# Weighted values of four steps in one block, six probability buffers, low queries in three buffers, maxima planned one step earlier

## The chip, the cores and the metric

The kernel runs on one core of one Trainium2 chip. The metric is the device time of one execution in microseconds (us), the median of several runs.

## The reference

A transformer block on x of 4 x 2048 x 512 in float32: layer norm with modulation, attention with 16 heads of 32 columns and 32 rotary columns shared by all heads, and a feed-forward part. What matters here is the attention:

```python
c_kv = x @ W_kv_down
k_rope = _rotary_apply(c_kv @ W_k_rope, cos, sin)
k = (c_kv @ W_k_up).reshape(Bb, Tt, NH, HD)
v = (c_kv @ W_v_up).reshape(Bb, Tt, NH, HD)
q = (x @ W_q).reshape(Bb, Tt, NH, HD)
q_rope = _rotary_apply(x @ W_q_rope, cos, sin)
scores = jnp.einsum('bqhd,bkhd->bhqk', q, k)
scores = scores + jnp.einsum('bqr,bkr->bqk', q_rope, k_rope)[:, None]
scores = scores / scale
causal = jnp.triu(jnp.ones((Tt, Tt), dtype=bool), k=1)
scores = jnp.where(causal[None, None], -jnp.inf, scores)
w = jax.nn.softmax(scores, axis=-1)
attn = jnp.einsum('bhqk,bkhd->bqhd', w, v).reshape(Bb, Tt, D_MODEL)
```

## The kernel before

The program has three stages one after the other: projection (modulation, layer norm, queries, keys and values, written to DRAM as high and low parts), attention, and feed-forward. The change touches attention alone.

Attention works on 16 units (`NU`), a unit being four heads of one batch. A unit has four chunks of 512 queries (`TCH`), j = 0 to 3, and chunk j has 4(j+1) steps of 128 keys each, so that a unit has 40 steps (`NSTEP`) and the kernel 640. They begin at `FIRST` = 0, 4, 12 and 24. The last four steps of each chunk lie on the diagonal and are 512, 384, 256 and 128 queries wide.

What one step t does:

- **PE, scores** (`scores`, L1194 and L1195). For each of the four heads two matmuls, of the high queries with high and low keys and of the low queries with the high keys. The low queries' buffer `q_b` has one row more, which holds minus the maximum of each query, so that the maximum is subtracted on the way. Three PSUM banks (`SBANKS`) take the scores.
- **ACT** (`exponentials`, L1035) writes the exponentials into one of five probability buffers (`RING`). It waits until PE's values and POOL's sum have read the step that had the buffer.
- **POOL** (`clear_future`, `add`) clears what lies behind the diagonal (L1115) and sums the probabilities of the steps that `SHARE_OF` marks with G into `sum_g` (L1130, L1131, L1134). The steps marked T are summed on PE instead.
- **PE, weighted values** (`weighted_values`, L1201). Each head's values fill 32 columns of the array, so four heads run side by side into `ps_o`; the steps marked T are run again with ones in place of the values, into `ps_d`. This work comes in blocks, `over_two_steps`: at each odd t a block for the steps t-3 and t-2 (`LAG` = 2).
- **The closing** (`close_denominators`), in the block two steps behind a chunk's last one: PE multiplies `sum_g` by ones into `ps_d`. At chunks 0, 2 and 3 it stands first in its block, at chunk 1 last. It needs POOL's last sum of the chunk, and POOL's first sum of the next chunk needs the closing (`closed`).
- **DVE behind the closing**: four reciprocals of `ps_d` (`invert`, L1084) and one scaling (`normalise`, L1088). They are entered in `extras` at fixed steps, two reciprocals at the first step behind the closing, two and the scaling at the second.

The maxima are found ahead of their use, by full-precision scores that are thrown away. PE makes a piece (`maximum`, L1178) of 128 queries by up to 512 keys into one of three banks (`MBANKS`), and DVE reduces it, a plain one at L1071, one on the diagonal at L1074. A piece's matmul waits until DVE has taken the piece three places before. A unit has 160 pieces; the last of a chunk is followed by a turn (L1166, L1065) and by a small DMA that places the maxima in `q_b` (`place_max`).

Where the pieces go is decided at build time. `maximum_plan` deals the pieces of unit u over pairs of steps from step 24 of the unit before to step 21 of its own. `deal` gives a pair a number of pieces that grows with `streams(m)`, PE's work in the pair in matmuls of 512 columns, less `CLOSING` in the pair that begins two steps behind a chunk's first one, where DVE has reciprocals to do:

```python
closes = lambda m: CLOSING * any(FIRST[j] + 2 == 2 * m for j in range(TCH))
share = lambda rho, m: max(0.0, (rho * streams(m) - closes(m)) / (PIECE - rho))
```

Within a step PE spreads the pieces behind its parts (four heads, and the block where there is one), and DVE spreads them between its extras, both in the same order. PE, DVE, ACT and POOL each run their list in order.

SP issues the loads in order, each behind a wait: a chunk's queries for the next unit when its scores are done. Each chunk j has its own `q_a[j]` and `q_b[j]`.

Of the kernel before, what the change touches and what calls it, by code (L numbers as in the profile page):

```python
# [22 lines left out]
P = 128  # L23
# [632 lines left out]
RING = 5  # L656
# [13 lines left out]
ENDS_ON_PE = [owners[-1] == "T" for owners in SHARE_OF]  # L670
OPENED_BY_SUM = ["T" not in owners.rstrip("T") for owners in SHARE_OF]
# [71 lines left out]
def maximum_plan():  # L743
# [3 lines left out]
    for u in range(NU):  # L747
# [14 lines left out]
    return plan  # L762

# [33 lines left out]
def operand_loads(sp, scratch, ops, k_b=None, kb_in=None):  # L797
# [34 lines left out]
def attention(nc, keep, scratch, ops, dram):  # L832


    with ExitStack() as ctx:
# [7 lines left out]
        ops["q_b"] += [sb(f"q_b{j}", [2 * HD + 1, GH, CH], F32R) for j in range(1, TCH)]  # L843
# [40 lines left out]
        assert NSTEP % RING == 0  # L884

# [37 lines left out]
        def _(sp):  # L923
            load_q_a, load_q_b, load_k_a, load_k_b, load_v, (heads, rotary) = operand_loads(sp, scratch, ops, k_b, kb_in)

            def load_q(u, j):
                load_q_a(u, j)
                load_q_b(u, j)

# [29 lines left out]
            def body(u, nxt):  # L959
                if u:  # L960
                    store_o(u - 1, TCH - 1)
                if nxt:
                    load_k_next(u + 1)
                    wait_alone(sp, scores_ready, GH * (NSTEP * u + STEPS[0]), sp_mark)
                    load_q(u + 1, 0)
# [17 lines left out]
                if nxt:  # L983
# [11 lines left out]
                    load_q(u + 1, TCH - 1)  # L995
# [9 lines left out]
            for j in range(2, TCH):  # L1005
                load_q(0, j)
# [96 lines left out]
        def _(pool):  # L1103
# [8 lines left out]
            def clear_future(u, j, i):  # L1112

                at = probs[(FIRST[j] + i) % RING][:, :, (i - TB * j) * P:(i - TB * j + 1) * P]
# [3 lines left out]
            def add(u, j, i, mine):  # L1118
                s = FIRST[j] + i
                c0 = CH - step_width(s)  # L1120
                new = probs[s % RING][:, :, c0:CH]
# [4 lines left out]
                if i == mine[1]:  # L1126
                    first = probs[(FIRST[j] + mine[0]) % RING]
# [22 lines left out]
        def _(pe):  # L1150
# [29 lines left out]
            def scores(u, j, i, hh):  # L1180
# [14 lines left out]
                last = mm(out[:, c0:CH], k_b[:, hh, i * P:(i + 1) * P], q_b[j][0:2 * HD + 1, hh, c0:CH], start=False, stop=True)  # L1195
# [11 lines left out]
            def weighted_values(u, j, i):  # L1207
# [11 lines left out]
                last = over_keys(ps_o, lambda hh: v[:, i // TB, i % TB, hh * HD:(hh + 1) * HD], probs[s % RING],  # L1219
                                 start=(i == 0), stop=(i == STEPS[j] - 1), c0=c0)  # L1220
                if SHARE_OF[j][i] == "T":
# [3 lines left out]
                    last = over_keys(ps_d, ones, probs[s % RING], start=first, stop=(i == STEPS[j] - 1), c0=c0)  # L1225
                last.then_inc(pv_done, 1)

            def close_denominators(u, j):
# [4 lines left out]
                last = over_keys(ps_d, ones, sum_g, start=opens, stop=not ENDS_ON_PE[j])  # L1233
# [545 lines left out]
```

## Time and profile before

| | |
|---|---|
| median of 3 runs | 3613.83 us (3613.76 to 3614.35) |
| the profiled execution's own time | 3614.24 us |
| its span, first to last instruction | 3612.5 us |
| mean granted TensorE clock | 0.992 |
| PE busy | 3494.5 us, 97% |
| DVE busy | 2562.3 us, 71% |
| ACT busy | 1820.9 us, 50% |
| POOL busy | 2673.0 us, 74% |

A matmul is recorded with its latency, so that the next starts before it ends: the time that one takes from PE is read from start to start, not from its duration. A float32 matmul in a block of weighted values is recorded twice, since it makes two passes; x16 is two steps of four heads.

### The profile page before, as it was taken

To read this page: it belongs to the slowest core of one execution; us is meant where nothing else is said; L and a number is where in the kernel's file an instruction comes from. 1 tells how busy PE (TensorE), PEld (TensorE's weight loads), DVE (VectorE), ACT (ScalarE), POOL (GpSimd) and SP (SyncE) were. 2 spreads that over 40 slices of the span, in tenths; PEclk is the share of its full clock that TensorE was granted. 3 is DMA by queue.
4 is the path that set the end of the run, shared out by engine and by line. 5 is a ranking of instruction groups with operands and counts; after the bars stand their busy time and mean duration, and the time that the engine had idled before them with its cause. 6 is when DMAs were issued, how large, how long until landed. Compare 5 with 4: busy or idle time off the path is not lost. (4 is left out here: it accounts for less than half of the span.)

```text
span 3612.5 us, 54216 instructions
## 1 busy us (share of the span) xinstructions
PE 3494.5 (97%) x19552; PEld 2416.0 (67%) x19552; DVE 2562.3 (71%) x5329; ACT 1820.9 (50%) x3455; POOL 2673.0 (74%) x1194
## 2 busy tenths in 40 slices
PE   8999989999999999999999999999999699999999
PEld 4777756666666666666666666666665488888887
DVE  6676677777777777777777777777775366666665
ACT  2333335555555555565555555555555344444443
POOL 2333349889898898898988989889889566666665
PEclk9999999999999999999999999999999899999999
DMA  5778773463534635536346354463551111212120
GB/s 203 272 271 306 254 175 76 104 145 74 134 86 108 138 82 115 120 92 138 83 100 149 76 124 98 97 141 79 114 132 60 62 59 70 70 70 71 70 70 36
DMA packets 232756, 426.58 MB, mean 118 GB/s; under 512 B 25380, under 2 KB 26916, under 8 KB 232488
## 3 DMA queue, kind: packets, MB, share of 16 engines
q1 hardware_dynamic: 232424, 423.10, 43.5%
q8 instruction: 155, 2.54, 0.3%
q14 instruction: 113, 0.93, 0.1%
q10 hardware_dynamic: 64, 0.02, 0.0%
HBM read 300.86 MB, written 121.65 MB: 117 GB/s over the span
## 5 line engine op out<-in xcount | busy, mean ns | idle before, releaser
L1035 ACT ACTIVATE att_probs<-att_ps_s 128x512 f32<-128x512 f32 (+3 forms) x2560 | 1309.3, 536 | 914.6 <-PE att_ps_s L1195 810.6
L1134 POOL TENSOR_TENSOR att_sum_g<-att_sum_g,att_probs 128x2048 f32<-128x2048 f32 (+3 forms) x400 | 1625.2, 4063 | 46.4 <-ACT att_probs L1035 1.7
L1071 DVE TENSOR_REDUCE att_piece_max<-att_ps_m 128x1 f32<-128x512 f32 x1520 | 963.3, 684 | 303.4 <-PE att_ps_m L1178 300.8
L1194 PE MATMUL att_ps_s<-att_q_a,att_k_a 128*128 128x512 f32 (+3 forms) x2560 | 952.3, 376 | 18.8 <-DMA att_q_b<-att_neg_max 9.0
L1195 PE MATMUL att_ps_s<-att_q_b,att_k_b 65*128 65x512 f32 (+3 forms) x2560 | 932.5, 368 | 0.0
L1074 DVE CUSTOM_DVE_ANT_0 att_ps_m<-att_ps_m,mask_qk 128x128 f32<-128x128 f32 x1008 | 477.7, 513 | 259.7 <-PE att_ps_m L1178 246.2
L1178 PE MATMUL att_ps_m<-att_k_a,att_q_a 128*128 128x512 f32 (+3 forms) x1808 | 643.6, 381 | 1.5 <-DVE att_piece_max L1071 0.9
L1194 PEld LDWEIGHTS att_ps_s<-att_q_a,att_k_a 128*128 128x128 f32 x2560 | 485.7, 190 | 158.3 <-issue 54.0
L1201 PE MATMUL att_ps_o<-att_probs,att_v 128*32 128x512 f32 (+3 forms) x5120 | 547.1, 536 | 4.2 <-POOL att_probs L1115 4.2
L1195 PEld LDWEIGHTS att_ps_s<-att_q_b,att_k_b 65*128 65x128 f32 x2560 | 484.5, 189 | 62.6
L1178 PEld LDWEIGHTS att_ps_m<-att_k_a,att_q_a 128*128 128x128 f32 x1808 | 336.6, 190 | 218.2 <-issue 116.1
L1131 POOL TENSOR_TENSOR att_sum_g<-att_probs 128x1536 f32<-128x1536 f32 (+1 forms) x64 | 276.5, 4321 | 120.1 <-PE att_ps_d L1201 120.1
L1201 PEld LDWEIGHTS att_ps_o<-att_probs,att_v 128*32 128x32 f32 x5120 | 139.3, 110 | 276.7 <-issue 162.1
L1084 DVE RECIPROCAL att_ps_d<-att_ps_d 128x128 f32<-128x128 f32 x256 | 222.0, 922 | 66.3 <-PE att_ps_d L1201 66.3
L1115 POOL TENSOR_SCALAR_AFFINE_SELECT att_probs<-att_probs 128x512 f32<-128x512 f32 x256 | 159.2, 636 | 135.5 <-ACT att_probs L1035 135.4
L1178 PE MATMUL att_ps_m<-att_k_next,att_q_a 128*128 128x128 f32 (+1 forms) x720 | 252.6, 381 | 0.0
L1178 PEld LDWEIGHTS att_ps_m<-att_k_next,att_q_a 128*128 128x128 f32 x720 | 135.2, 189 | 83.8 <-issue 28.1
L513 POOL TENSOR_TENSOR prj_h_lo<-prj_h_f,prj_h_hi 128x512 fp32r<-128x512 f32 x64 | 84.2, 1342 | 114.6 <-ACT prj_h_hi L450 114.6
L1389 DVE TENSOR_TENSOR ffn_x<-ffn_ps_ffn,ffn_gate 128x512 f32<-128x512 f32 x64 | 44.2, 691 | 172.5 <-PE ffn_ps_ffn L62 172.5
L1550 ACT ACTIVATE ffn_act_f<-ffn_relu 128x512 f32<-128x512 f32 x64 | 40.5, 632 | 249.0 <-DVE ffn_relu L1462 248.9
L1074 DVE DVE_READ_ACCUMULATOR2_ANT att_piece_max<- 128x1 f32 x1008 | 143.2, 142 | 0.0
L1525 ACT CAST att_q_a<-ffn_ps_t 128x512 fp32r<-128x512 f32 x128 | 75.2, 588 | 128.7 <-DVE ffn_ps_t L1430 127.7
(189 smaller groups left out, 4951.5 us busy)
## 6 DMA issues: line engine op xcount, KB each, us to landing
att_q_a<-s_q_hi SPq DMA_DIRECT2D x128, 256.0 KB, 6.0
att_q_a<-s_qr_hi SPq DMA_DIRECT2D x128, 256.0 KB, 6.6
prj_x_sb<-in_x_dram SPq DMA_DIRECT2D x16, 1024.0 KB, 5.2
s_q_hi<-prj_q_hi SPq DMA_DIRECT2D x16, 1024.0 KB, 4.2
s_q_lo<-prj_q_lo SPq DMA_DIRECT2D x16, 1024.0 KB, 6.0
s_k_hi<-prj_k_hi SPq DMA_DIRECT2D x16, 1024.0 KB, 4.4
s_k_lo<-prj_k_lo SPq DMA_DIRECT2D x16, 1024.0 KB, 6.4
s_v<-prj_v_sb SPq DMA_DIRECT2D x16, 1024.0 KB, 9.1
```

The lines of the kernel that those rows point to most:

```text
L513: pool.tensor_tensor(h[1][:, c, :], h_f[:, c, :], as_f32(h[0][:, c, :]), ALU.subtract).then_inc(hlo_ready, 1)
L1035: act.activation(probs[t % RING][:, hh, c0:CH], ps_s[(GH * t + hh) % SBANKS][:, c0:CH], ACT.Exp, scale=SCALE).then_inc(probs_ready, 1)
L1071: dve.tensor_reduce(top, ps_m[:, bank, :], AX_X, ALU.max).then_inc(piece_taken, 1)
L1074: dve.tensor_tensor_reduce(ps_m[:, bank, 0:width], ps_m[:, bank, 0:width], keep["mask_qk"][:, CH - width:CH], 1.0, MASKED, ALU.add, ALU.ma ...
L1084: dve.reciprocal(cols, cols).then_inc(rden_ready, 1)
L1115: pool.affine_select(out=at, in_=at, compare_op=ALU.is_ge, fill=0.0, base=0, pattern=[[0, GH], [1, P]], channel_multiplier=-1).then_inc(cl ...
L1131: pool.tensor_tensor(sum_g[:, :, c0:CH], first[:, :, c0:CH], new, ALU.add).then_inc(sum_added, 1)
L1134: pool.tensor_tensor(sum_g[:, :, c0:CH], sum_g[:, :, c0:CH], new, ALU.add).then_inc(sum_added, 1)
L1178: mm(ps_m[:, bank, 0:width], q_a[j][:, hh, r * P:(r + 1) * P], keys, start=True, stop=True).then_inc(piece_ready, 1)
L1194: mm(out[:, c0:CH], k_a[:, hh, i * P:(i + 1) * P], q_a[j][:, hh, c0:CH], start=True, stop=False)
L1195: last = mm(out[:, c0:CH], k_b[:, hh, i * P:(i + 1) * P], q_b[j][0:2 * HD + 1, hh, c0:CH], start=False, stop=True)
L1201: last = mm(out[hh * HD:(hh + 1) * HD, c0:CH], stat(hh), mov[:, hh, c0:CH], start=start, stop=stop, skip_group_check=True)
```

## The change

- `TOGETHER` = 4: a block (`over_four_steps`) holds four steps, t-5 to t-2, and comes at every fourth step, t = 5, 9, 13 and so on. A chunk's steps fill whole blocks.
- The closing is last in its block at all four chunks. `ENDS_ON_PE` goes.
- `RING` = 6; the buffer of a step is now taken from its number over all units.
- `QB_RING` = 3: `low_queries(u, j)` gives chunk (u, j) one of three `q_b` buffers in turn (the last chunk of all gets number 1). Low queries are loaded one chunk later than before: those of chunk 3 when the scores of chunk 0 of the same unit are done, those of the next unit's chunks 0, 1 and 2 behind chunks 1, 2 and 3. `q_a` stays at four.
- `streams` counts the values in the pair at whose end the block stands, at most 9 matmuls of them.
- `plan[t - 1 if u else t]`: all pieces of the units from 1 on stand one step earlier than they are dealt. `closes` and DVE's `extras` stay as they are.

```diff
-RING = 5
+RING = 6
+TOGETHER = 4
+QB_RING = 3
...
-ENDS_ON_PE = [owners[-1] == "T" for owners in SHARE_OF]
-OPENED_BY_SUM = ["T" not in owners.rstrip("T") for owners in SHARE_OF]
+OPENED_BY_SUM = ["T" not in owners for owners in SHARE_OF]
...
     own = sum(2 * GH * step_width(s) for s in (2 * m, 2 * m + 1))
-    due = [(2 * m - 2) % NSTEP, (2 * m - 1) % NSTEP]
+    due = [(2 * m - n) % NSTEP for n in range(1, TOGETHER + 1)] if 2 * m % TOGETHER == 0 else []
+    values = 0
     for s in due:
         j = max(j for j in range(TCH) if FIRST[j] <= s)
-        own += GH * step_width(s) * (2 if SHARE_OF[j][s - FIRST[j]] == "T" else 1)
-    return own / CH + GH * any(FIRST[j] == (2 * m) % NSTEP for j in range(TCH))
+        values += GH * step_width(s) * (2 if SHARE_OF[j][s - FIRST[j]] == "T" else 1)
+    return (own + min(values, VALUES_MOST * CH)) / CH
+
+VALUES_MOST = 9
...
             for t, some in deal(items, pairs).items():
-                plan[t] += some
+                plan[t - 1 if u else t] += some
...
+def low_queries(u, j):
+
+    return 1 if (u, j) == (NU - 1, TCH - 1) else (TCH * u + j) % QB_RING
...
                     wait_alone(sp, scores_ready, GH * (NSTEP * u + STEPS[0]), sp_mark)
-                    load_q(u + 1, 0)
+                    load_q_a(u + 1, 0)
+                    load_q_b(u, 3)
...
                     wait_alone(sp, scores_ready, GH * (NSTEP * u + FIRST[1] + STEPS[1]), sp_mark)
-                    load_q(u + 1, 1)
+                    load_q_a(u + 1, 1)
+                    load_q_b(u + 1, 0)
                 else:
+                    wait_alone(sp, scores_ready, GH * (NSTEP * u + FIRST[1] + STEPS[1]), sp_mark)
+                    load_q_b(u, 3)
                     load_for_last_stage(1)
...
-            def over_two_steps(t, closing):
-
-                if closing and ENDS_ON_PE[closing[1]]:
-                    close_denominators(*closing)
-                for due in (t - LAG - 1, t - LAG):
+            def over_four_steps(t, closing):
+
+                for due in range(t - LAG - TOGETHER + 1, t - LAG + 1):
                     weighted_values(*STEP_OF[due])
-                if closing and not ENDS_ON_PE[closing[1]]:
+                if closing:
                     close_denominators(*closing)
...
-                if t > LAG and t % 2 == 1:
-                    parts.append(lambda: over_two_steps(t, closing))
+                if t > LAG and (t - LAG) % TOGETHER == TOGETHER - 1:
+                    parts.append(lambda: over_four_steps(t, closing))
```

How the plan moves, in pieces for each step of a unit in mid-kernel (turns counted in):

| steps | before | after |
|---|---|---|
| 0 to 7 | 5 6 0 0 6 6 1 1 | 6 0 0 7 6 1 0 7 |
| 8 to 15 | 5 5 3 3 5 6 0 1 | 6 1 2 6 7 0 0 7 |
| 16 to 23 | 5 6 5 6 5 5 1 0 | 6 5 4 6 6 1 0 7 |
| 24 to 31 | 6 5 1 0 6 6 6 5 | 6 0 0 7 7 5 4 7 |
| 32 to 39 | 7 6 6 5 5 6 4 4 | 6 4 5 6 6 2 2 6 |

The blocks stand at the end of every odd step before, and at the end of steps 1, 5, 9 and so on after; the closings at the end of steps 1 (chunk 3), 5, 13 and 25 in both.

Three places in the order of the instructions show it. First PE at the closing of chunk 1 (`att_ps_d<-att_sum_g`), before:

```order
L1178 MATMUL att_ps_m<-att_k_a,att_q_a 128x512
L1201 MATMUL att_ps_o<-att_probs,att_v 32x256 x4
L1201 MATMUL att_ps_o<-att_probs,att_v 32x128 x4
L1201 MATMUL att_ps_d<-att_sum_g,ones 32x512 x4
L1178 MATMUL att_ps_m<-att_k_a,att_q_a 128x512 x2
L1194 MATMUL att_ps_s<-att_q_a,att_k_a 128x512
```

and after:

```order
L1203 MATMUL att_ps_s<-att_q_b,att_k_b 128x512
L1209 MATMUL att_ps_o<-att_probs,att_v 32x512 x4
L1209 MATMUL att_ps_o<-att_probs,att_v 32x384 x4
L1209 MATMUL att_ps_o<-att_probs,att_v 32x256 x4
L1209 MATMUL att_ps_o<-att_probs,att_v 32x128 x4
L1209 MATMUL att_ps_d<-att_sum_g,ones 32x512 x4
L1202 MATMUL att_ps_s<-att_q_a,att_k_a 128x512
```

The block has four steps, and no piece (`att_ps_m`) stands right before or behind it any more.

Second PE two steps behind that closing, before:

```order
L1194 MATMUL att_ps_s<-att_q_a,att_k_a 128x512
L1195 MATMUL att_ps_s<-att_q_b,att_k_b 128x512
L1201 MATMUL att_ps_o<-att_probs,att_v 32x512 x8
L1178 MATMUL att_ps_m<-att_k_a,att_q_a 128x512
L1194 MATMUL att_ps_s<-att_q_a,att_k_a 128x512
L1195 MATMUL att_ps_s<-att_q_b,att_k_b 128x512
L1178 MATMUL att_ps_m<-att_k_a,att_q_a 128x512
```

and after, from the last head of the first step behind the closing:

```order
L1202 MATMUL att_ps_s<-att_q_a,att_k_a 128x512
L1203 MATMUL att_ps_s<-att_q_b,att_k_b 128x512
L1202 MATMUL att_ps_s<-att_q_a,att_k_a 128x512
L1203 MATMUL att_ps_s<-att_q_b,att_k_b 128x512
L1186 MATMUL att_ps_m<-att_k_a,att_q_a 128x512
L1202 MATMUL att_ps_s<-att_q_a,att_k_a 128x512
L1203 MATMUL att_ps_s<-att_q_b,att_k_b 128x512
L1186 MATMUL att_ps_m<-att_k_a,att_q_a 128x512 x2
L1202 MATMUL att_ps_s<-att_q_a,att_k_a 128x512
L1203 MATMUL att_ps_s<-att_q_b,att_k_b 128x512
L1186 MATMUL att_ps_m<-att_k_a,att_q_a 128x512 x2
```

The second step behind the closing had no piece but the one behind its block; it now has seven.

Third DVE from the closing of chunk 0 to that of chunk 1, before (`TENSOR_REDUCE att_piece_max` is a piece, `TENSOR_SCALAR` a turn):

```order
L1078 TENSOR_REDUCE att_row_max<-att_piece_max 128x16
L1071 TENSOR_REDUCE att_piece_max<-att_ps_m 128x1 x3
L1084 RECIPROCAL att_ps_d<-att_ps_d 128x128 x2
L1065 TENSOR_SCALAR att_neg_max<-att_ps_m 16x128
L1084 RECIPROCAL att_ps_d<-att_ps_d 128x128 x2
L1088 TENSOR_TENSOR att_o_sb<-att_o_sb,att_ps_d 128x512
L1071 TENSOR_REDUCE att_piece_max<-att_ps_m 128x1 x28
L1084 RECIPROCAL att_ps_d<-att_ps_d 128x128 x4
L1088 TENSOR_TENSOR att_o_sb<-att_o_sb,att_ps_d 128x512
```

and after:

```order
L1086 TENSOR_REDUCE att_row_max<-att_piece_max 128x16
L1079 TENSOR_REDUCE att_piece_max<-att_ps_m 128x1
L1073 TENSOR_SCALAR att_neg_max<-att_ps_m 16x128
L1092 RECIPROCAL att_ps_d<-att_ps_d 128x128 x2
L1079 TENSOR_REDUCE att_piece_max<-att_ps_m 128x1
L1092 RECIPROCAL att_ps_d<-att_ps_d 128x128
L1079 TENSOR_REDUCE att_piece_max<-att_ps_m 128x1 x2
L1092 RECIPROCAL att_ps_d<-att_ps_d 128x128
L1079 TENSOR_REDUCE att_piece_max<-att_ps_m 128x1 x2
L1096 TENSOR_TENSOR att_o_sb<-att_o_sb,att_ps_d 128x512
L1079 TENSOR_REDUCE att_piece_max<-att_ps_m 128x1 x24
L1092 RECIPROCAL att_ps_d<-att_ps_d 128x128 x2
```

The reciprocals of a chunk stood together; the second pair and the scaling now stand among the seven pieces of the step.

## Rows read from the trace of the kernel before

**Rows 1.** The page: span, busy time of each engine, clock in 40 slices.

```profile
span 3612.5 us, 54216 instructions
...
PE 3494.5 (97%) x19552; PEld 2416.0 (67%) x19552; DVE 2562.3 (71%) x5329; ACT 1820.9 (50%) x3455; POOL 2673.0 (74%) x1194
...
PEclk9999999999999999999999999999999899999999
```

**Rows 2.** Busy time in one period of attention: stretch and length, engines (instructions), clock, DMA.

```profile
core 0: us, PE busy (x) PEld busy (x) DVE busy (x) ACT busy (x) POOL busy (x), PEclk, DMA share, GB/s
1526.50:1672.80 146.30, 143.94 (x896) 92.95 (x894) 109.88 (x253) 84.39 (x164) 128.85 (x46) 1.00 0.47 109
```

**Rows 3.** Waits of PE, whole kernel: who for whom, us, times, longest.

```profile
PE att_ps_d L1201 <- POOL att_sum_g L1134: 37.5, 31, 2.8
...
PE att_ps_s L1194 <- DMA att_q_b<-att_neg_max: 9.0, 5, 6.6
```

**Rows 4.** Who waited for DVE's maxima (`att_piece_max`), whole kernel: us, times.

```profile
  PEld att_ps_m L1178: 73.4, 172
```

**Rows 5.** Timeline of PE round a block: start, us, instruction, count [idle before].

```profile
1511.66 0.34 PE L1195 MATMUL att_ps_s<-att_q_b,att_k_b 65*128 65x384 f32 x1
1511.83 0.39 PE L1178 MATMUL att_ps_m<-att_k_a,att_q_a 128*128 128x512 f32 x1
1512.15 1.92 PE L1201 MATMUL att_ps_o<-att_probs,att_v 128*32 128x512 f32 x16
1514.01 0.74 PE L1178 MATMUL att_ps_m<-att_k_a,att_q_a 128*128 128x512 f32 x2
1514.59 0.28 PE L1194 MATMUL att_ps_s<-att_q_a,att_k_a 128*128 128x256 f32 x1
```

**Rows 6.** Timeline of PE at the closings of chunks 0, 1 and 2, unit 7.

```profile
1538.56 1.07 PE L1201 MATMUL att_ps_d<-att_sum_g,ones 128*32 128x512 f32 x8
...
1568.36 1.07 PE L1201 MATMUL att_ps_d<-att_sum_g,ones 128*32 128x512 f32 x8 [1.26 <-POOL att_sum_g L1134]
1569.36 0.73 PE L1178 MATMUL att_ps_m<-att_k_a,att_q_a 128*128 128x512 f32 x2
...
1610.84 1.06 PE L1201 MATMUL att_ps_d<-att_sum_g,ones 128*32 128x512 f32 x8 [1.09 <-POOL att_sum_g L1134]
```

**Rows 7.** Timeline of POOL over chunks 1 and 2, unit 7.

```profile
1539.82 4.58 POOL L1131 TENSOR_TENSOR att_sum_g<-att_probs 128x2048 f32<-128x2048 f32 x1 [3.83 <-PE att_ps_d L1201]
...
1560.77 7.45 POOL L1134 TENSOR_TENSOR att_sum_g<-att_sum_g,att_probs 128x1536 f32<-128x1536 f32 x3
1569.59 4.61 POOL L1131 TENSOR_TENSOR att_sum_g<-att_probs 128x2048 f32<-128x2048 f32 x1 [1.38 <-PE att_ps_d L1201]
...
1604.76 6.03 POOL L1134 TENSOR_TENSOR att_sum_g<-att_sum_g,att_probs 128x1536 f32<-128x1536 f32 x2
1612.08 4.61 POOL L1131 TENSOR_TENSOR att_sum_g<-att_probs 128x2048 f32<-128x2048 f32 x1 [1.30 <-PE att_ps_d L1201]
```

**Rows 8.** DVE: a run of pieces, one closing (timeline), and reciprocals of the period by shape.

```profile
1514.55 3.08 DVE L1071 TENSOR_REDUCE att_piece_max<-att_ps_m 128x1 f32<-128x512 f32 x5 [1.10 <-PE att_ps_m L1178]
...
1569.89 1.29 DVE L1071 TENSOR_REDUCE att_piece_max<-att_ps_m 128x1 f32<-128x512 f32 x2 [2.85 <-PE att_ps_m L1178]
1571.10 3.39 DVE L1084 RECIPROCAL att_ps_d<-att_ps_d 128x128 f32<-128x128 f32 x4
1574.52 0.69 DVE L1088 TENSOR_TENSOR att_o_sb<-att_o_sb,att_ps_d 128x512 f32<-128x512 f32 x1
...
L1071 DVE TENSOR_REDUCE att_piece_max<-att_ps_m 128x1 f32<-128x512 f32 x96 | 60.9, 685 | 19.1 <-PE att_ps_m L1178 18.9
L1084 DVE RECIPROCAL att_ps_d<-att_ps_d 128x128 f32<-128x128 f32 x16 | 13.8, 922 | 0.0
```

**Rows 9.** Timeline of PE: a head and a piece at full width.

```profile
1521.87 0.39 PE L1178 MATMUL att_ps_m<-att_k_a,att_q_a 128*128 128x512 f32 x1
1522.10 0.39 PE L1194 MATMUL att_ps_s<-att_q_a,att_k_a 128*128 128x512 f32 x1
1522.33 0.40 PE L1195 MATMUL att_ps_s<-att_q_b,att_k_b 65*128 65x512 f32 x1
1522.56 0.40 PE L1178 MATMUL att_ps_m<-att_k_a,att_q_a 128*128 128x512 f32 x1
```

**Rows 10.** The page's group of ACT's exponentials: count, busy us, mean ns of one, idle before.

```profile
L1035 ACT ACTIVATE att_probs<-att_ps_s 128x512 f32<-128x512 f32 (+3 forms) x2560 | 1309.3, 536 | 914.6 <-PE att_ps_s L1195 810.6
```

More of the change, by code:

```diff
@@ L812, in load_q_b @@
         for row, src in ((0, heads["q_lo"][i]), (HD, rotary("qr_lo", i))):
-            sp.dma_start(as_f32(ops["q_b"][j][row:row + HD, :, :]), src).then_inc(ops["qb_in"][j], 16)
+            sp.dma_start(as_f32(ops["q_b"][low_queries(u, j)][row:row + HD, :, :]), src).then_inc(ops["qb_in"][j], 16)
     def load_k_a(u, j):
@@ L842, in attention @@
         ops["q_a"].append(sb("q_a3", [P, GH, CH], F32R))
-        ops["q_b"] += [sb(f"q_b{j}", [2 * HD + 1, GH, CH], F32R) for j in range(1, TCH)]
+        ops["q_b"] += [sb(f"q_b{j}", [2 * HD + 1, GH, CH], F32R) for j in range(1, QB_RING)]
         q_a, q_b = ops["q_a"], ops["q_b"]
@@ L978, in body @@
                     wait_alone(sp, scores_ready, GH * (NSTEP * u + FIRST[2] + STEPS[2]), sp_mark)
-                    load_q(u + 1, 2)
+                    load_q_a(u + 1, 2)
+                    load_q_b(u + 1, 1)
                 else:
@@ L994, in body @@
                     load_k_a(u + 1, TCH - 1)
-                    load_q(u + 1, TCH - 1)
+                    load_q_a(u + 1, TCH - 1)
+                    load_q_b(u + 1, 2)
                     load_k_b(u + 1, TCH - 1)
@@ L1005, in _ @@
             for j in range(2, TCH):
-                load_q(0, j)
+                load_q_a(0, j)
+                if j < QB_RING:
+                    load_q_b(0, j)
                 load_k_b(0, j)
@@ L1112, in clear_future @@
             def clear_future(u, j, i):
[L1114 removed]
+                at = probs[(NSTEP * u + FIRST[j] + i) % RING][:, :, (i - TB * j) * P:(i - TB * j + 1) * P]
                 pool.affine_select(out=at, in_=at, compare_op=ALU.is_ge, fill=0.0, base=0, pattern=[[0, GH], [1, P]],
@@ L1120, in add @@
                 c0 = CH - step_width(s)
-                new = probs[s % RING][:, :, c0:CH]
+                new = probs[(NSTEP * u + s) % RING][:, :, c0:CH]
                 if i >= TB * j:
@@ L1126, in add @@
                 if i == mine[1]:
-                    first = probs[(FIRST[j] + mine[0]) % RING]
+                    first = probs[(NSTEP * u + FIRST[j] + mine[0]) % RING]
                     pool.wait_ge(closed, TCH * u + j + 1)
@@ L1194, in scores @@
                 mm(out[:, c0:CH], k_a[:, hh, i * P:(i + 1) * P], q_a[j][:, hh, c0:CH], start=True, stop=False)
-                last = mm(out[:, c0:CH], k_b[:, hh, i * P:(i + 1) * P], q_b[j][0:2 * HD + 1, hh, c0:CH], start=False, stop=True)
+                last = mm(out[:, c0:CH], k_b[:, hh, i * P:(i + 1) * P], q_b[low_queries(u, j)][0:2 * HD + 1, hh, c0:CH], start=False, stop=True)
                 last.then_inc(scores_ready, 1)
@@ L1218, in weighted_values @@
                     pe.wait_ge(v_in[j], 16 * u + 16)
-                last = over_keys(ps_o, lambda hh: v[:, i // TB, i % TB, hh * HD:(hh + 1) * HD], probs[s % RING],
+                last = over_keys(ps_o, lambda hh: v[:, i // TB, i % TB, hh * HD:(hh + 1) * HD], probs[(NSTEP * u + s) % RING],
                                  start=(i == 0), stop=(i == STEPS[j] - 1), c0=c0)
@@ L1224, in weighted_values @@
                         pe.wait_ge(o_ready, TCH * u + j + 1)
-                    last = over_keys(ps_d, ones, probs[s % RING], start=first, stop=(i == STEPS[j] - 1), c0=c0)
+                    last = over_keys(ps_d, ones, probs[(NSTEP * u + s) % RING], start=first, stop=False, c0=c0)
                 last.then_inc(pv_done, 1)
@@ L1232, in close_denominators @@
                 pe.wait_ge(sum_added, summed(u, j, SHARE_OF[j].rindex("G")))
-                last = over_keys(ps_d, ones, sum_g, start=opens, stop=not ENDS_ON_PE[j])
+                last = over_keys(ps_d, ones, sum_g, start=opens, stop=True)
                 last.then_inc(closed, 1)
-            def over_two_steps(t, closing):
-                if closing and ENDS_ON_PE[closing[1]]:
-                    close_denominators(*closing)
-                for due in (t - LAG - 1, t - LAG):
+            def over_four_steps(t, closing):
+                for due in range(t - LAG - TOGETHER + 1, t - LAG + 1):
                     weighted_values(*STEP_OF[due])
-                if closing and not ENDS_ON_PE[closing[1]]:
+                if closing:
                     close_denominators(*closing)
```

10 lines of the change are left out of this document (2 added, 8 removed).

## The prediction

> **What bounds the kernel now.** I read the page first: the span is 3612.5 us, the profiled execution's own time 3614.24 us, the median of the three runs 3613.83 us, so a sum made against the profile stands 0.4 us above the median. PE is busy 97% of the span, and its clock row stays at 9 tenths or more but for one 8 [rows 1]. Attention covers about two thirds of it and repeats almost exactly: from one unit to the next the closing of the last chunk comes 146.3 us later. I therefore read one such period, unit 7. In it PE is busy 143.9 us of 146.3, DVE 109.9, POOL 128.9, at clock 1.00 [rows 2]. The missing 2.4 us are two waits of a closing for POOL's sum; the list of waits has 37.5 us of them in 31 pieces over the kernel [rows 3]. Nothing else stops PE visibly. But the weight loads on PE's side stood 73.4 us for DVE's maxima [rows 4]: three banks of scores for the maximum stand between PE and DVE, and they are only just enough.
>
> **Blocks (a gain).** Weighted values use 32-column tiles, all else in attention the full array. What does one change to the tiles and back cost? The piece before a block starts at 1511.83, the second piece behind it at 1514.35 (1514.59 less one spacing of 0.234), that is 2.52 us [rows 5]. The block's four passes of 512 columns take 0.429 each (two steps fill 1.72), the two pieces 0.234 each, together 2.18. The price is 0.33 us a block. The change makes 160 blocks of 320: 160 x 0.33 = -53 us. The Trainium skill, TensorEngine Tiling, Key Properties, says that a change of tiling mode drains TensorE, without a figure; by the drains alone, the start of the block (0.32 instead of 0.23) and its end (0.11), the gain would be 32 us, and the trace adds 0.10 us because the first full-array piece after a block starts 0.34 before its follower, and 0.02 in the first pass.
>
> **The closing last (a gain).** PE's waits for POOL were 1.26 us at the closing of chunk 1 and 1.09 us at that of chunk 2 [rows 6]. POOL's sums run without a break for 28.4 us from 1539.82 to 1568.22 and for 41.2 us from 1569.59 to 1610.79, and POOL starts again 1.24 us after each closing starts [rows 7]. These chains alone fix 29.8 us from closing 0 to closing 1 (1538.56 to 1568.36) and 42.5 us from there to closing 2 (1610.84), 72.3 in all, whatever PE does. If PE gets slower than that there, the waits vanish: -35 us. If it gets faster, they grow. So what PE gains in chunks 1 and 2 is worth nothing; a loss there costs only what exceeds about 2.4 us.
>
> **Six buffers, low queries in three.** With four steps in a block, the block that ends step t holds steps t-5 to t-2; the exponential of step t+1 needs the buffer of t-5, which the block has just read. Six is the least that doesn't stop ACT, and POOL has a step more. I take 0; the cover is ACT's slack (84.4 of 146.3 us [rows 2]). The low queries of chunk 3 are now loaded after chunk 0 and needed twenty steps later, those of the next unit's chunk 0 after chunk 1, 28 steps ahead: SP issues the same transfers, with the waits of before but for one that the last unit now has twice. Bounds: the rows waited for today cost 9.0 us in 5 waits [rows 3]; between 0 and 9 us, I take 0 because four of the five together are 2.4 us (9.0 less one of 6.6).
>
> **Maxima one step ahead (the loss).** The planner still keeps the pair of steps free that DVE needs for the four reciprocals and the scaling, but the whole list is written one step earlier while DVE's reciprocals stay. Before, DVE met the reciprocals with three pieces or fewer near them [rows 8]. Now the free steps are the one before the block and the one after it. DVE idles beside the block, and two reciprocals and the scaling fall in a step with seven pieces. Durations: a piece every 0.60 us when DVE sets the pace (five in 3.08, so (3.08-0.68)/4), a reciprocal 0.83 ((3.39-0.92)/3, 0.92 being one alone), the scaling 0.59 to 0.69 [rows 8]; on PE a head of scores 0.47 and a piece 0.234 [rows 9].
> Closing 1, from PE's first score behind it. PE alone: 1.98 for the step without pieces (with 0.10 after the block), 3.51 for four heads and seven pieces, 3.27 for four heads and six; the last piece is issued 8.5 us in. DVE: two reciprocals are done in time; the first piece lands at 2.95, then reciprocal, two pieces, reciprocal, two, scaling, two: 2.95 + 7 x 0.60 + 2 x 0.83 + 0.59 = 9.4. The thirteenth piece needs the bank of the tenth: 9.4 + 3 x 0.60 = 11.2, and 0.1 until PE sees it. PE stands 11.3 - 8.5 = 2.8 us. Closing 0 has the same counts. At closing 2 three of seven pieces are masked (shorter on both engines), at closing 3 the heads are narrow; laid out alike they give 3.1 and 2.8. I take 2.8 for each: 11.2 us a unit.
> Away from closings DVE needs 7 x 0.60 = 4.2 us against PE's 3.5 in a step with seven pieces, since in four steps 22 or 23 pieces must go where PE isn't in a longer block. The banks absorb some of it. Laid out like the closing, steps 11 and 12, 23, 31 and 32, 35 and 36, 39 and 0 leave 1.4 + 0.9 + 0.7 + 0.3 + 1.0 = 4.3 us; the order before, laid out alike, has 1.3. Net 3.0 us a unit.
> All four closings and these steps are met in 15 units' worth (the last unit has no next one): 15 x (11.2 + 3.0) = +213 us. Against that loss: PE's real pace outside waits is 1.6 us a unit slower than the durations laid end to end (143.9 against 142.3, of which 1.3 is DVE's), and time spent thus beside a late DVE is no longer extra: -24 us. In chunks 1 and 2 PE's path becomes 30.6 + 44.2 us against POOL's 29.8 + 42.5, so POOL's waits are gone and nothing of the loss is hidden twice.
>
> **Sum.** 3614.2 - 53 - 35 + 213 - 24 = 3715 us. The tail adds under 2 us (reciprocals now start behind the last block), left out.
>
> **Rivals.**
> A, DVE keeps up. If DVE's stalls add up to under 5.9 us a unit (88 us over 15), the change is faster, and it decides at about 1.2 us a closing with nothing elsewhere. Then POOL's chain binds from closing 0 to closing 2, and only the rest counts: 74.0 us before, less 5 blocks x 0.33, less 0.86 (values of chunk 2 now ahead of its closing), plus 1.29 (values of chunk 0 likewise), less three pieces (74 stood between closing 0 and closing 2, now 77) x 0.234: 72.1. Gain 1.9 us a unit, 15.5 units: 3585 us. For it: DVE is busy 110 of 146 us, a quarter is free. Against it: that is an average; the free time lies beside the blocks.
> B, half the stalls: DVE 7.1 us a unit, 3614 - 53 - 35 + 106 = 3632 us. It would need pieces well under 0.60; no row shows that where DVE sets the pace.
> C, all of it and more: nothing is absorbed (3739), and rows of low queries come late for up to twice today's 9 us: 3755 us. For it: SP waits in order, and a placement behind a store now waits for scaling that comes later.
> D, the larger block starves ACT, so that PE meets its three score banks full afterwards: 0.54 us a head on ACT [rows 10] against 0.47 on PE over eight heads without pieces is 0.5 us, within the three banks; 160 x 0.5 would be 80 us more. Little speaks for it.
>
> **Numbers.** The main case 0.76, C and D 0.05, B 0.07, A 0.09, no change 0.03. Faster 0.09, same 0.03, slower 0.88; 0.2% (7 us) is about what a measurement of this kernel can tell. The range runs from just under B to C, 3625 to 3755, and leaves out A, no change and D.
>
> **What would show it.** Right: blocks of 32 passes with 0.33 us round them, 160 of them; no PE wait for POOL's sum at closings 1 and 2; DVE idle 4 us and more beside each block, then back to back for 20 pieces' worth; the period per unit near 153 us; PE standing for att_piece_max in the second and third step behind every closing, some 2.8 us; weight loads' wait for DVE several times 73 us. The blocks' term is wrong if the block's surroundings shrink by other than 0.33. The loss is wrong if DVE's reciprocals run beside the block, or if periods of the unit come out under 146.3; then A holds, and closings 1 and 2 still wait for POOL.

## The result and the profile after

The changed kernel takes 3832.36 us (median of 4 runs, 3829.95 to 3836.89) against 3613.8 us of the kernel before on the same chip: 1.0606 times as long, 95% interval 1.0593 to 1.0619. Slower was forecast, but 3715 us, and 3832 lies outside the range of 3625 to 3755. The direction and the main mechanism came true; the loss of 219 us is over twice the 101 that was forecast.

Lines of the page of the changed kernel that answer to [rows 1] and [rows 10], and that of POOL's first sums:

```profile
span 3831.2 us, 54200 instructions
...
PE 3617.0 (94%) x19552; PEld 2440.6 (64%) x19552; DVE 2536.0 (66%) x5329; ACT 1799.9 (47%) x3455; POOL 2670.5 (70%) x1194
...
L1043 ACT ACTIVATE att_probs<-att_ps_s 128x512 f32<-128x512 f32 (+3 forms) x2560 | 1288.4, 536 | 1097.6 <-PE att_ps_s L1203 1043.9
...
L1139 POOL TENSOR_TENSOR att_sum_g<-att_probs 128x1536 f32<-128x1536 f32 (+1 forms) x64 | 276.1, 4313 | 237.1 <-PE att_ps_d L1209 237.1
```

ACT, DVE and POOL do the work of before and only wait longer; POOL's idle time before a chunk's first sum is 237 us, where it was 120. PE is busy 94% of a span that is 6% longer. So the time is PE's, and it stands for others. Its busy time is 122 us longer for the same 19552 matmuls; part of that is a lower clock, as the steps below show. Its waits, whole kernel, which answer to [rows 3], and who waited for DVE's maxima, which answers to [rows 4]:

```profile
PE att_ps_m L1186 <- DVE att_piece_max L1079: 58.6, 78, 1.1
...
PE att_ps_m L1186 <- DMA att_k_a<-s_kr_lo: 26.5, 15, 3.0
PE att_ps_s L1202 <- DMA att_q_b<-att_neg_max: 9.8, 2, 8.2
...
  PEld att_ps_m L1186: 314.3, 560
  PE att_ps_m L1186: 91.8, 140
```

The wait for POOL's sum is gone from closings 1 and 2, as forecast. In its place PE itself stands 92 us for DVE, and its weight loads 314 us where it was 73. The row of `att_k_a` was not forecast at all: 15 waits for a DMA of keys, 26.5 us.

A period, unit 7, and pieces of unit 9, against [rows 2]: the whole period, then steps 3, 4, 7 and 8.

```profile
1625.50:1785.90 160.40, 150.77 (x856) 94.34 (x851) 108.23 (x252) 82.66 (x164) 128.00 (x45) 0.96 0.41 95
...
1952.30:1956.60 4.30, 2.68 (x17) 2.06 (x17) 4.30 (x14) 1.58 (x6) 3.49 (x3) 1.00 1.08 216
1956.60:1961.20 4.60, 4.60 (x16) 3.79 (x16) 3.58 (x14) 2.08 (x4) 1.70 (x2) 0.63 1.06 257
1968.90:1974.60 5.70, 4.33 (x17) 2.93 (x16) 5.05 (x9) 3.19 (x6) 5.55 (x2) 0.96 0.31 63
1974.60:1979.20 4.60, 4.60 (x16) 3.65 (x15) 4.16 (x7) 2.07 (x4) 4.46 (x2) 0.68 0.17 62
```

The last three columns are the granted clock, DMA share and GB/s. The period is about 160.4 us, not 153. In step 3 DVE is busy all of 4.30 us and PE 2.68: PE stands for DVE. In step 4 PE is busy throughout, at a granted clock of 0.63: most of the step runs at 1.2 GHz, the lower of the two levels. The clock row of the page hides this, since a slice of it is over 90 us long. By the trace's clock records attention, up to the last unit's last step, has 157 us at half clock, where before it had 10.

The duration of each step, read from the starts of its first score matmul (median of units 3 to 13), in us. "Laid out" is an estimate: the order of the instructions with the durations of the prediction, worked out for every step in the way in which the prediction did it for closing 1.

| step | laid out | measured | more |
|---|---|---|---|
| 3 | 4.49 | 4.31 | -0.2 |
| 4 | 3.16 | 4.53 | 1.4 |
| 7 | 5.42 | 5.42 | 0.0 |
| 8 | 4.18 | 4.78 | 0.6 |
| 14, 15, 16 | 1.98, 5.42, 4.18 | 1.99, 5.41, 4.18 | 0.0 |
| 27, 28 | 5.17, 4.57 | 5.26, 4.48 | 0.0 |
| 33 | 7.09 | 10.65 | 3.6 |
| all other 30 steps, each | | | about 0 to 0.3 |

DVE behind the closing of chunk 1, timeline, which answers to [rows 8]:

```profile
1674.15 1.78 DVE L1092 RECIPROCAL att_ps_d<-att_ps_d 128x128 f32<-128x128 f32 x2 [3.87 <-PE att_ps_d L1209]
1676.93 0.69 DVE L1079 TENSOR_REDUCE att_piece_max<-att_ps_m 128x1 f32<-128x512 f32 x1 [1.00 <-PE att_ps_m L1186]
1677.54 0.96 DVE L1092 RECIPROCAL att_ps_d<-att_ps_d 128x128 f32<-128x128 f32 x1
1678.40 1.22 DVE L1079 TENSOR_REDUCE att_piece_max<-att_ps_m 128x1 f32<-128x512 f32 x2
1679.54 0.96 DVE L1092 RECIPROCAL att_ps_d<-att_ps_d 128x128 f32<-128x128 f32 x1
1680.40 1.22 DVE L1079 TENSOR_REDUCE att_piece_max<-att_ps_m 128x1 f32<-128x512 f32 x2
1681.54 0.68 DVE L1096 TENSOR_TENSOR att_o_sb<-att_o_sb,att_ps_d 128x512 f32<-128x512 f32 x1
1682.13 7.26 DVE L1079 TENSOR_REDUCE att_piece_max<-att_ps_m 128x1 f32<-128x512 f32 x12
```

PE's first score behind the closing starts at 1674.01. The prediction had DVE done with the scaling and two more pieces 9.4 us later; here it is 1682.13 + 2 x 0.6 - 1674.01 = 9.3. PE in the same place:

```profile
1678.12 0.40 PE L1186 MATMUL att_ps_m<-att_k_a,att_q_a 128*128 128x512 f32 x1
1679.08 0.50 PE L1186 MATMUL att_ps_m<-att_k_a,att_q_a 128*128 128x512 f32 x1 [0.56 <-DVE att_piece_max L1079]
...
1681.08 0.50 PE L1186 MATMUL att_ps_m<-att_k_a,att_q_a 128*128 128x512 f32 x1 [0.79 <-DVE att_piece_max L1079]
```

The three steps 14 to 16 take 11.6 us where PE alone would need 8.8: the stall of 2.8 that was worked out. Of it 0.56 + 0.79 us show as waits of matmuls; the rest stands in the weight loads before them.

Step 33, unit 7, where the first diagonal piece of the next unit's chunk 1 is due:

```profile
1748.87 0.40 PE L1203 MATMUL att_ps_s<-att_q_b,att_k_b 65*128 65x512 f32 x1
1752.28 0.45 PE L1186 MATMUL att_ps_m<-att_k_a,att_q_a 128*128 128x128 f32 x1 [3.01 <-DMA att_k_a<-s_kr_lo]
1752.52 0.73 PE L1202 MATMUL att_ps_s<-att_q_a,att_k_a 128*128 128x512 f32 x1
1753.05 0.63 PE L1203 MATMUL att_ps_s<-att_q_b,att_k_b 65*128 65x512 f32 x1
1753.48 0.41 PE L1186 MATMUL att_ps_m<-att_k_a,att_q_a 128*128 128x256 f32 x1
```

The keys of the next unit's chunk 1 are loaded over those of this unit once step 31 has used them. The piece is due two steps later, and these two steps have no block between them any more. The 3.0 us of this row are the longest of the 15 waits; their mean is 1.8. And behind the wait matmuls of 512 columns start 0.43 us apart where it was 0.23 [rows 9]: half clock again.

A block of four, unit 7, against [rows 5]:

```profile
1688.16 0.39 PE L1186 MATMUL att_ps_m<-att_k_a,att_q_a 128*128 128x512 f32 x1
1688.48 3.64 PE L1209 MATMUL att_ps_o<-att_probs,att_v 128*32 128x512 f32 x32
1692.06 0.50 PE L1186 MATMUL att_ps_m<-att_k_a,att_q_a 128*128 128x512 f32 x1
1692.39 0.39 PE L1202 MATMUL att_ps_s<-att_q_a,att_k_a 128*128 128x512 f32 x1
```

From 1688.16 to 1692.39 are 4.23 us. Eight passes of 0.429 and two spacings of 0.234 make 3.90, and 0.33 is left, as round a block of two. Read so from both traces, the median is 0.325 us in 127 full-width blocks of two before and 0.328 in 32 full-width blocks of four after. The price of a block does not grow with its length.

### The profile page after: what moved, and what is told of

Its sections match the earlier page's. It is cut to its first block and busy times, and to the rows that moved or that the text cites. A ratio compares the mean times of both kernels' runs of the same rounds, so it can differ in the third digit from the quotient of the medians.

```text
span 3831.2 us, 54200 instructions
## 1 busy us (share of the span) xinstructions
PE 3617.0 (94%) x19552; PEld 2440.6 (64%) x19552; DVE 2536.0 (66%) x5329; ACT 1799.9 (47%) x3455; POOL 2670.5 (70%) x1194
## 5 line engine op out<-in xcount | busy, mean ns | idle before, releaser
L1043 ACT ACTIVATE att_probs<-att_ps_s 128x512 f32<-128x512 f32 (+3 forms) x2560 | 1288.4, 536 | 1097.6 <-PE att_ps_s L1203 1043.9
L1079 DVE TENSOR_REDUCE att_piece_max<-att_ps_m 128x1 f32<-128x512 f32 x1520 | 947.2, 681 | 225.0 <-PE att_ps_m L1186 220.4
L1202 PE MATMUL att_ps_s<-att_q_a,att_k_a 128*128 128x512 f32 (+3 forms) x2560 | 970.9, 382 | 17.4 <-DMA att_q_b<-att_neg_max 9.8
L1203 PE MATMUL att_ps_s<-att_q_b,att_k_b 65*128 65x512 f32 (+3 forms) x2560 | 951.5, 374 | 0.0
L1186 PE MATMUL att_ps_m<-att_k_a,att_q_a 128*128 128x512 f32 (+3 forms) x1808 | 677.6, 404 | 101.7 <-DVE att_piece_max L1079 42.5
L1186 PEld LDWEIGHTS att_ps_m<-att_k_a,att_q_a 128*128 128x128 f32 x1808 | 355.7, 198 | 336.8 <-DVE att_piece_max L1079 154.6
L1092 DVE RECIPROCAL att_ps_d<-att_ps_d 128x128 f32<-128x128 f32 x256 | 235.0, 943 | 272.4 <-PE att_ps_d L1209 272.4
L1209 PEld LDWEIGHTS att_ps_o<-att_probs,att_v 128*32 128x32 f32 x5120 | 153.1, 112 | 326.2 <-issue 256.1
L1186 PE MATMUL att_ps_m<-att_k_next,att_q_a 128*128 128x128 f32 (+1 forms) x720 | 271.0, 402 | 27.5 <-DVE att_piece_max L1079 16.0
L1073 DVE TENSOR_SCALAR att_neg_max<-att_ps_m 16x128 fp32r<-16x128 f32 x63 | 17.3, 275 | 181.6 <-PE att_ps_m L1174 181.6
```

Of the source, the lines that this page charges most:

```text
L1043: act.activation(probs[t % RING][:, hh, c0:CH], ps_s[(GH * t + hh) % SBANKS][:, c0:CH], ACT.Exp, scale=SCALE).then_inc(probs_ready, 1)
L1079: dve.tensor_reduce(top, ps_m[:, bank, :], AX_X, ALU.max).then_inc(piece_taken, 1)
L1092: dve.reciprocal(cols, cols).then_inc(rden_ready, 1)
L1186: mm(ps_m[:, bank, 0:width], q_a[j][:, hh, r * P:(r + 1) * P], keys, start=True, stop=True).then_inc(piece_ready, 1)
L1202: mm(out[:, c0:CH], k_a[:, hh, i * P:(i + 1) * P], q_a[j][:, hh, c0:CH], start=True, stop=False)
L1209: last = mm(out[hh * HD:(hh + 1) * HD, c0:CH], stat(hh), mov[:, hh, c0:CH], start=start, stop=stop, skip_group_check=True)
```

## The experiments

The question was how 219 us are shared: by pieces that meet the reciprocals, by the wait for keys, by the clock, and whether the step earlier or the longer block is to blame. All times are medians, and each ratio is to the kernel before on the same chip (its medians there are 3612.5 to 3613.8 us).

**Other keys for the diagonal pieces of chunk 1.** They read `k_next`, which has long been loaded.

```diff
-            return u > 0 and j < TCH - 1 and kc == 0
+            return u > 0 and (j < TCH - 1 and kc == 0 or (j, kc) == (1, 1))
```

> The change, but the 16 diagonal pieces of chunk 1 read their keys from k_next, which is loaded long before, in place of k_a; their maxima are taken over other keys, everything else is the same. Theory: PE's wait of 3.0 us for the DMA of att_k_a in step 33 goes, and the half clock behind it. Step 33 is 3.6 us longer than its durations laid end to end in 14 or 15 units: 3832 - 53 = 3779 us, and the stretches at half clock in step 33 are gone while those of steps 4 and 8 stay. Rival (DVE would have stopped PE there anyway): 3820 us or more.

Measured: 3780.87 us, ratio 1.0459 (1.0444 to 1.0475). The wait is not in the list any more, and no stretch at half clock is left in step 33; those of step 4 stay in 15 units. The wait and what followed it cost 51 us: 26.5 of standing, and about 25 of half clock behind it. That fits the clock records of the change: the stretches at half clock that begin in step 33 are 51 us long in all, and half of such time is lost where PE sets the pace.

**Short reciprocals.** Eight columns in place of 128; the other denominators are not inverted, so the result is not that of the reference.

```diff
-                cols = ps_d[:, r * P:(r + 1) * P]
+                cols = ps_d[:, r * P:r * P + 8]
```

> The change, but each of DVE's four reciprocals of a chunk works on 8 columns in place of 128, so that most denominators are not inverted. Theory: behind a closing PE stands for DVE because two reciprocals and the scaling fall among seven pieces. With reciprocals of some 0.15 us the layout of durations loses 70 us, and the half clock in steps 4 and 8 goes with it, some 30 us more: 3730 us (3710 to 3760). The wait for att_k_a and the half clock in step 33 stay. Rival (the seven pieces alone are too many, the reciprocals don't matter): 3820 us.

Measured: 3722.27 us, ratio 1.0301 (1.0285 to 1.0316), 110 us less than the change. No half clock is left in steps 4 and 8, that in step 33 stays. PE's waits of this kernel:

```profile
PE att_ps_m L1186 <- DMA att_k_a<-s_kr_lo: 26.9, 15, 2.7
...
PE att_ps_m L1186 <- DVE att_piece_max L1082: 9.0, 32, 0.3
PE att_ps_m L1186 <- DVE att_piece_max L1079: 5.3, 16, 0.3
```

PE's 92 us for DVE are down to 14, but its weight loads still stand 252 us for DVE where they stood 314. By steps, over 15 units, 78 us went in the steps 3, 7, 15 and 27, where the second pair of reciprocals runs, and 24 in the steps 4 and 8 with the half clock. The steps 15 and 16 are 3.97 and 4.18 us long, where the prediction has 3.51 and 3.27 for PE alone. So about half of a closing's stall of 2.8 us comes from the reciprocals and the other half stays without them: six or seven pieces a step are more than DVE can take at 0.60 us each.

**Both at once.**

> Both at once, other keys for the diagonal pieces of chunk 1 and reciprocals of 8 columns. Theory: the two losses are in different steps and add up: 3832 - 53 - 100 = 3679 us, with hardly any half clock left in attention. Rival (one of them hides behind the other): within 20 us of the better of the two alone.

Measured: 3668.95 us, ratio 1.0154 (1.0137 to 1.0171). 51 + 110 = 161 were to go, and 163 went: two separate losses. What is left over the kernel before is 55 us, with 17 us at half clock in attention where the kernel before has 10; PE's weight loads still wait 219 us for DVE, in the dense steps behind the closings as in those away from them.

**The clock by itself.** In the steps 3 and 7 PE makes each piece twice, which fills the time in which it stands for DVE.

```diff
-            def maximum(item):
+            def maximum(item, twice=False):
...
+                if twice:
+                    mm(ps_m[:, bank, 0:width], q_a[j][:, hh, r * P:(r + 1) * P], keys, start=True, stop=True)
                 mm(ps_m[:, bank, 0:width], q_a[j][:, hh, r * P:(r + 1) * P], keys, start=True, stop=True).then_inc(piece_ready, 1)
...
-                        maximum(it)
+                        maximum(it, t % NSTEP in (3, 7))
```

> The change, but PE makes each piece of the steps 3 and 7 of a unit twice in a row, the second time over the first (the second alone is announced). PE stands for DVE in these steps, so the 14 more matmuls a unit fit beside the stall: the layout of durations has 3 us more over the kernel. Theory: the half clock of steps 4 and 8 comes from PE having been idle much of the step before; with its idle time filled the stretches there go and step 4 falls from 4.5 to some 3.1 us, step 8 from 4.8 to 4.1: 3832 - 30 + 3 = 3805 us. Rival (the clock falls for another reason, or more matmuls don't matter to it): 3835 us, stretches at half clock as before.

Measured: 3805.29 us, ratio 1.0535 (1.0518 to 1.0553): 27 us faster, with more matmuls and nothing else changed. The same four steps as above, unit 9:

```profile
1933.00:1937.60 4.60, 3.62 (x24) 2.99 (x24) 4.56 (x14) 1.60 (x6) 3.79 (x3) 1.00 1.06 212
1937.60:1940.70 3.10, 3.10 (x16) 2.44 (x15) 3.05 (x13) 2.00 (x4) 1.40 (x2) 1.00 1.05 274
1948.50:1954.40 5.90, 5.56 (x23) 4.07 (x23) 5.02 (x9) 3.17 (x6) 5.75 (x2) 1.00 0.49 103
1954.40:1958.30 3.90, 3.81 (x15) 2.46 (x14) 3.90 (x7) 2.17 (x4) 3.76 (x2) 1.00 0.20 74
```

PE is busy 3.62 of 4.60 us in step 3, where it was 2.68 of 4.30, and the clock stays at 1.00 in step 4, which takes 3.1 us and not 4.6. The extra matmuls cost 0.3 us in step 3 and 0.5 in step 7 (medians of units 3 to 13). Over 15 units the steps 4 and 8 are 28 us shorter and the steps 3 and 7 are 10 us longer. This shows that the clock there followed how much PE had stood still, and that it cost some 30 us at these two places. Of the 27 us gained another 10 come from step 33, where nothing was changed: its waits for keys are the same (28.1 us in 15), but 8 stretches at half clock follow them and not 14. Why, no run here shows.

**The step earlier undone.**

```diff
-                plan[t - 1 if u else t] += some
+                plan[t] += some
```

> The change with its maxima not moved one step earlier; blocks of four, closing last, six buffers, three low-query buffers and the new streams stay. Theory (the step earlier is what costs: pieces meet the reciprocals, the first pieces on the diagonal of chunk 1 meet the load of the next unit's keys, and both stalls let the clock fall): all three go at once. Durations laid along the order give 5 us less than before over attention, so 3609 us, between 3600 and 3620; no wait of PE for att_k_a, hardly any time at half clock in attention, PE waiting for POOL's sum again at closings 1 and 2 (some 50 us in all). Rival (the denser dealing or the longer block itself starves DVE and PE): still 3700 us or more.

Measured: 3717.68 us, ratio 1.0287 (1.0271 to 1.0302). It gave back 115 us and not 223, and the expectation was wrong by 109. The wait for keys and the half clock of steps 4, 8 and 33 did go, and PE's own waits for DVE fell from 92 to 31 us, but other losses came. Its waits, and steps 22 to 24 of unit 9:

```profile
PE att_ps_s L1202 <- DMA att_q_b<-att_neg_max: 32.0, 18, 8.5
PE att_ps_d L1209 <- POOL att_sum_g L1142: 21.5, 16, 1.5
PE att_ps_m L1186 <- DVE att_piece_max L1082: 20.9, 32, 1.2
```

```profile
1957.35 0.27 PE L1174 MATMUL att_ps_m<-ident_f,att_row_max 128*16 128x128 f32 x1 [0.27 <-DVE att_row_max L1086]
...
1958.32 0.28 PE L1203 MATMUL att_ps_s<-att_q_b,att_k_b 65*128 65x128 f32 x1
1959.92 0.76 PE L1202 MATMUL att_ps_s<-att_q_a,att_k_a 128*128 128x512 f32 x1 [1.32 <-DMA att_q_b<-att_neg_max]
1960.48 0.63 PE L1203 MATMUL att_ps_s<-att_q_b,att_k_b 65*128 65x512 f32 x1
```

The turn of chunk 3 stands behind the scores of step 22, and its row is needed at step 24. Before, the block at the end of step 23 lay between them; with blocks of four there is none, two narrow steps of 128 to 256 columns pass in 3 us, and the row lands too late. Nearly every unit waits, and the clock falls there: 147 us of attention at half clock, 92 of them in stretches that begin in steps 23 and 24. So with blocks of four the maxima of chunk 3 come too late in the plan of before, and one step earlier for all pieces brings them in time at a larger price.

**The blocks with the plan of before.** Old `streams`, nothing earlier.

```diff
-    due = [(2 * m - n) % NSTEP for n in range(1, TOGETHER + 1)] if 2 * m % TOGETHER == 0 else []
+    due = [(2 * m - 2) % NSTEP, (2 * m - 1) % NSTEP]
...
-                plan[t - 1 if u else t] += some
+                plan[t] += some
```

> The blocks of four, closing last, six buffers and three low-query buffers with the plan of before (old streams, nothing moved a step earlier). Theory A (after the look at e1: with no block at step 23 the row of maxima of chunk 3 lands 1.5 us late for step 24, and narrow steps without a block let the clock fall): PE waits for att_neg_max in nearly every unit, 20 to 30 us in all, half clock comes in steps 23 and 24, and the kernel takes 3640 to 3700 us although 160 changes of tiling are gone. Theory B (the dense new dealing is at fault in e1): within 10 us of before.

Measured: 3677.79 us, ratio 1.0194 (1.0164 to 1.0223).

```profile
PE att_ps_d L1208 <- POOL att_sum_g L1141: 39.8, 16, 2.6
PE att_ps_s L1201 <- DMA att_q_b<-att_neg_max: 30.3, 18, 7.8
PE att_ps_m L1185 <- DVE att_piece_max L1081: 19.2, 15, 1.3
```

Theory A of the expectation holds. The late row is there without the dense dealing, and POOL's wait is now 39.8 us in 16 waits, some 2.5 us at each closing of chunk 1: what PE saves in chunk 1 it waits there, as the prediction's section on the closing had it. 96 us of attention are at half clock. Blocks of four don't pay in this kernel with either dealing.

**The step earlier alone, in the kernel before.**

> The kernel before with its maxima one step earlier and nothing else. Theory: the plan of before deals 5 or 6 pieces a step, and its blocks come every second step, so the step that meets the reciprocals is mild: the layout of durations has 9 us more, without the wait for att_k_a; with that wait (the first diagonal pieces of chunk 1 in step 33 or earlier) up to 45 us more: 3620 to 3660 us. Rival (the step earlier is bad by itself): over 3700 us.

Measured: 3636.24 us, ratio 1.0064 (1.0049 to 1.0079): 23 us. It has one wait for `att_k_a`, of 1.0 us, and not 15; with a block at step 31 the keys arrive in time.

**The change with blocks of two.** Its plan, its step earlier, its closing and buffers.

```diff
-                for due in range(t - LAG - TOGETHER + 1, t - LAG + 1):
+                for due in (t - LAG - 1, t - LAG):
...
-                if t > LAG and (t - LAG) % TOGETHER == TOGETHER - 1:
+                if t > LAG and t % 2 == 1:
```

> The change with everything but the blocks: its plan (dealt as if blocks held four), one step earlier, closing last, six buffers, three low-query buffers, but blocks of two steps at every odd step. It tells whether the plan one step earlier is bad by itself or together with the long blocks. Theory (together: with a block every second step PE gives DVE time right where the seven pieces are, and step 32 is long enough for the keys to land): the layout of durations has 15 us more than before over attention, stalls for DVE are 78 us where the change has 250, and PE's idle times are too short for the clock to fall: 3600 to 3650 us. Rival (the plan alone does it): over 3750 us.

Measured: 3642.76 us, ratio 1.0085 (1.0068 to 1.0102). Half clock in attention is 10 us, as before the change. The change differs from this kernel in nothing but the length of its blocks, and it is 190 us slower, although it has 160 blocks fewer, which are worth 53 us. The plan one step earlier costs 30 us here, so it is not free by itself, but the large loss needs the long blocks with it: with a block every second step DVE catches up where it has fallen behind (PE waits 6.9 us for it, not 92), the keys make PE wait once for 1.0 us, and the clock doesn't fall.

**The free steps moved to the reciprocals.** With the other keys of the first experiment.

```diff
-    closes = lambda m: CLOSING * any(FIRST[j] + 2 == 2 * m for j in range(TCH))
+    closes = lambda m: CLOSING * any((FIRST[j] + 4) % NSTEP == 2 * m for j in range(TCH))
```

> As e3 (other keys for the diagonal pieces of chunk 1), and the planner's nearly free pair moved by two steps, so that after the shift it covers the steps 3 and 4 behind a chunk's first one, where the second pair of reciprocals and the scaling run. Nothing else is left out. Theory (the collision of pieces and reciprocals is the largest loss): the layout of durations has 75 us less than the change, and the half clock of steps 4 and 8 goes: 3781 - 75 - 30 = 3676 us (3650 to 3700). Rival (DVE is too slow for this dealing wherever the free pair is): 3760 us or more.

Measured: 3661.48 us, ratio 1.0132 (1.0117 to 1.0147), 119 us less than the first experiment, though all reciprocals are full here: most of what the pieces cost is gone once they keep out of DVE's way behind a closing. It is still 1.3% slower than the kernel before. The form that would read the right keys as well has its first diagonal piece of chunk 1 in step 32, a step earlier still, and would be expected to wait longer for them; it wasn't tried.

**A version that beats both.** The kernel before, with three of POOL's sums on PE.

```diff
-SHARE_OF = ("GGTT", "GGGGGGGG", "GGGGGGGGTGGT", "GGGGGGTGGGGGTGGT")
+SHARE_OF = ("GGTT", "GGGGGGTT", "GGGGGGGGTGTT", "GGGGGGTGGGGGTGGT")
```

> The kernel before with three of POOL's sums given to PE (steps 6 and 7 of chunk 1, step 10 of chunk 2): SHARE_OF is GGTT, GGGGGGTT, GGGGGGGGTGTT, GGGGGGTGGGGGTGGT. Theory: POOL's chain fixes the time from closing 0 to closing 2; without 3.6 and 2.4 us of it PE's 35 us of waits go, and PE pays 0.43 + 0.22 + 0.43 us a unit, 17 us: 3614 - 35 + 17 = 3596 us. Rival (POOL's waits only move to the next closing): 3614 us or more.

Measured: 3583.44 us, ratio 0.9919 (0.9905 to 0.9934), 29 us faster than before. Of the wait for `att_sum_g` one is left:

```profile
PE att_ps_d L1201 <- POOL att_sum_g L1134: 2.7, 1, 2.7
```

It is 13 us faster than the sum of the two terms had it. PE's busy time rose by 5 us (3494.5 to 3499.6) and not by the 17 that the sums given to it were to cost, so it is that term which was too large; why is not shown.

## Why the prediction was right or wrong

- **Blocks, -53 us.** Right: the surroundings of a block cost 0.33 us whether it holds two steps or four, so 160 blocks fewer give 53. No run has the gain alone.
- **The closing last, -35 us.** Right: no closing but the last of all waits for POOL.
- **Six buffers and low queries, 0.** Right: waits for `att_neg_max` are 9.8 us where they were 9.0, and PE itself waits 0.7 us for ACT.
- **Maxima one step ahead, +213 us.** The stalls for DVE were sized right; steps 14 to 16 agree to 0.03 us. The step of the working that failed is the one that counted DVE alone as the price of moving the pieces one step ahead. It left two costs at nothing. First, the keys: the diagonal pieces of chunk 1 were moved against the load they need, and I had followed the low queries' transfers but not the keys'. That is 51 us with the half clock behind it. Second, the clock: it was 1.00 in the period read [rows 2], and the sum took it for given, while the stalls that the sum itself forecast were what would bring it down. That is some 30 us at steps 4 and 8, as the experiment with pieces made twice shows.
- **The 24 us taken off** because PE is slower than its laid-out durations were wrong. By the table the steps in which DVE holds PE at full clock (7, 15, 16, 27 and 28) are within 0.1 us of what was laid out, so nothing was absorbed there.
- Put together: 3614 - 53 - 35 + 213 = 3739, + 51 for the keys, + 30 for the clock at steps 4 and 8 = 3820, against 3832 measured. The 12 that are left have not been taken apart.
- **Rivals.** A fell with POOL's waits, and B with the stalls of 2.8 us. C named late transfers, but for the rows of low queries, and priced them at 16 us (3755 against 3739). D fell too: for score banks that ACT has not freed PE stands 0.7 us and its weight loads 51 us, where they stood 42. What the prediction said would show it came as said (DVE's idle time beside the block is 3.9 us), but for the period, 160.4 and not 153. It had no sign for a wait for keys, nor one for the clock of the steps behind a stall.

## What to carry to other kernels

When work is moved earlier, list what each moved instruction reads and what frees the place it is loaded to; here a wait in each of 15 units, 1.8 us in the mean and 3.0 at most, came from keys that nobody had moved. A stall of an engine that sets the pace is to be priced with the clock that it may bring down: here some 147 us more than before ran at half clock, and in the repeating part of attention none of the waits in front of them was over 3.0 us. And lengthening a block to save its fixed price can take away the small pauses in which others catch up or a transfer lands: with one plan, blocks of four took 190 us more than blocks of two.

## What the runs showed of the hardware

TensorE's clock fell behind many short waits, without a long idle stretch. In step 3 PE was busy 62% of the time (2.68 of 4.30 us), its longest single wait for DVE in the kernel was 1.1 us, and step 4 ran at a granted 0.63; with step 3 filled up to 79% busy (3.62 of 4.60 us) step 4 ran at 1.00. The Trainium skill, TensorE: Matmul & The Clock Gate, Why this matters for your kernels, asks that bursts of matmuls not be parted by long idle gaps; here many short ones were enough, and the measurement decides. Matmuls whose results are thrown away, put beside the stalls, made the kernel 27 us faster, 18 of them in the four steps concerned.

The change from 128-column to 32-column tiles and back cost 0.33 us, whether two steps or four stood between (0.325 and 0.328 us, medians of both traces).
